# Second join and node stage in one pass, forward sums in the joins, first nodes' rows scattered during the lists

## The chip, the cores and the metric

The kernel runs on one core of a Trainium2 chip. The metric is the device time of one execution in microseconds (us). The engines are named as in the profile: PE (matmuls and transposes; PEld its weight loads), DVE (VectorE), ACT (ScalarE), POOL (GpSimd), SP (a queue that issues DMAs). Time before: 3021.86 us, the median of 3 runs (3020.35 to 3023.98).

## The reference, cut to what matters

```python
h = relu(x)                                        # 6250 nodes x 256
h = relu(gat_conv(h, src, dst, edge_attr, ...1))   # 106250 edges sorted by dst, 8 heads
h = gat_conv(h, src, dst, edge_attr, ...2)
x = h + x                                          # plus a mixing branch of the normalised x
# gat_conv: alpha = leaky_relu(a_src[src] + a_dst[dst] + a_edge); softmax over the edges of one dst;
#           out[dst] = sum(xp[src] * alpha) + bias
# then: y = layernorm(x); logits = relu(y @ rw1 + rb1) @ rw2 + rb2; the best two of 6 experts per
#       node, each a three-layer network of width 256; their weighted sum is added to x
```

The kernel computes all of it: two attention layers over the edges, the mixing branch, a router and the experts.

## The kernel before, in words

Edges are cut into T = 832 tiles of 128 (P), in the order of their destination, and nodes into 50 blocks of 128 or NCH = 25 chunks of 256 (CH). The kernel is a row of stages; each is a block in which every engine has an instruction list of its own, semaphores order the engines, and the next block starts when all have ended.

- `first`: layer norm of x, the rows of layer 1 (`table[0]`), and all constants, among them `begins` (1 where a tile's list starts anew for a destination), `ends_sep`, `ends_same` and `fix_rows`, the first destination of each tile. Small extra pieces are hung on DVE behind certain chunks (`pieces`).
- `edges` (twice): gathers a row for each edge, softmax within a tile, sums per destination into `acc`. Because a destination can lie on two or more tiles, each tile leaves its first and last destination's partial maximum and sum in `ends` and partial outputs in `parts`. In layer 2 this stage also leaves `base`, what has to be added to each node.
- `join` (twice): joins the partial results over tiles. PE picks `ends` into 8 rows (one a head) of L = 1664 entries (`pick`), ACT copies them out (`picked`), DVE scans forward and backward for the maxima (L1456, L1458), ACT takes the exponential (L1438), DVE makes `weight`, scans forward for the denominators and backward to carry the total to all entries (L1469, L1471), inverts, multiplies the outputs' parts by the weights (L1479), scans them forward (L1484), cuts (L1487), scans backward (L1489), copies (L1491), and multiplies by the inverse (L1496). Beside this the chunks of `acc` pass: ACT adds the bias (`biased`, L1413), PE projects them with the next layer's weights (layer 0) or only transposes them (layer 1), ACT copies rows (L1422), POOL splits the scores (layer 0) or adds `base` (layer 1, L1297), SP stores. PE's list puts the spreads (`spread`, L1334), which wait for DVE, between loops over chunks. Last come the first nodes of the tiles (`fix`): T rows in NFIX = 7 groups are projected (L1393), completed, and scattered over the stored rows by 7 indirect DMAs (L1314), which wait for all stores. A destination that is the first of several tiles is written several times, with the same values.
- `front`: the node stage. SP fetches a chunk of `node`, DVE takes its statistics (L1591, L1594), POOL the power -0.5 (L1583), DVE normalises both blocks (L1601), SP stores them, PE transposes (L1644), multiplies (L1653), and makes logits (L1660) with ACT's copies between; the router's weights are four small loads on ACT's queue.
- `dispatch`, the lists: the best two experts of a node, and for each expert the list of its nodes; SP loads the experts' weights and then stores two weights per node into `node` (L1741).
- `experts`: gathers the nodes' rows by these lists, runs the networks, scatters.

The order is written out by hand; no planner sets it.

## Time and profile before

| what | value |
|---|---|
| median of 3 runs | 3021.86 us |
| profiled execution | 3012.53 us, span 3010.7 us |
| mean granted PE clock | 0.892 of full speed |
| busy share of the span | PE 77%, DVE 72%, POOL 67%, ACT 39% |
| costliest group | POOL L702 (gathers for edges), 1583.6 us busy |
| second group | PE L1086 (sums over edges), 1106.0 us busy |

Busy time is the time in which an engine worked on instructions. "Idle before" stands in brackets behind a row of a timeline, with what ended it. Rows of a timeline begin with the start in us from the span's start and the busy time in us.

### The profile page before, as it was taken

To read this page: it belongs to the slowest core of one execution; us is meant where nothing else is said; L and a number is where in the kernel's file an instruction comes from. 1 tells how busy PE (TensorE), PEld (TensorE's weight loads), DVE (VectorE), ACT (ScalarE), POOL (GpSimd) and SP (SyncE) were. 2 spreads that over 40 slices of the span, in tenths; PEclk is the share of its full clock that TensorE was granted. 3 is DMA by queue.
4 is the path that set the end of the run, shared out by engine and by line. 5 is a ranking of instruction groups with operands and counts; after the bars stand their busy time and mean duration, and the time that the engine had idled before them with its cause. 6 is when DMAs were issued, how large, how long until landed. Compare 5 with 4: busy or idle time off the path is not lost. (4 is left out here: it accounts for less than half of the span.)

```text
span 3010.7 us, 76172 instructions
## 1 busy us (share of the span) xinstructions
PE 2320.1 (77%) x15555; PEld 1916.9 (64%) x15556; DVE 2170.8 (72%) x6026; ACT 1174.4 (39%) x4767; POOL 2026.9 (67%) x2248
## 2 busy tenths in 40 slices
PE   6577888888888888857777777777777756499897
PEld 4466666666666666636666666666666636387786
DVE  7477778777877777638777777777778686766565
ACT  3244444444444445413333333333333453322222
POOL 4577777777777775577777777777777473166665
PEclk9799999999999999868898898888889857599999
DMA  8765655555655553255655655665656356444432
GB/s 259 208 171 154 172 159 167 168 170 156 172 168 158 166 168 99 72 143 169 177 169 165 179 166 173 176 173 161 175 164 174 105 166 192 119 155 154 121 116 85
DMA packets 295431, 478.77 MB, mean 159 GB/s; under 512 B 69780, under 2 KB 211500, under 8 KB 295364
## 3 DMA queue, kind: packets, MB, share of 16 engines
q0 software_dynamic: 96704, 287.77, 33.6%
q1 hardware_dynamic: 134340, 143.68, 16.5%
q10 hardware_dynamic: 64320, 46.56, 4.9%
q8 instruction: 26, 0.43, 0.1%
q14 instruction: 41, 0.34, 0.0%
HBM read 405.02 MB, written 74.87 MB: 159 GB/s over the span
## 5 line engine op out<-in xcount | busy, mean ns | idle before, releaser
L702 POOL DMA_INDIRECT e_rows<-table,e_idx x1664 | 1583.6, 952 | 555.5 <-issue 396.5
L1086 PE MATMUL e_ps_sum<-e_hot,e_msg 128*128 128x129 f32 x6656 | 1106.0, 303 | 270.0 <-DVE e_msg L743 215.2
L1086 PEld LDWEIGHTS e_ps_sum<-e_hot,e_msg 128*128 128x128 f32 x6656 | 909.9, 203 | 429.2 <-ACT parts L941 239.5
L940 ACT ACTIVATE acc<-e_ps_sum 128x256 f32 x1664 | 640.5, 385 | 1222.2 <-PE e_ps_sum L1086 1036.7
L743 DVE TENSOR_TENSOR e_msg<-e_rows,e_ps_pr 128x256 f32<-128x256 f32 x1664 | 653.4, 413 | 80.6 <-issue 12.5
L722 DVE TENSOR_TENSOR e_hot<-e_ps_pr,rel 128x512 f32<-128x512 f32 x416 | 284.9, 685 | 160.0 <-PE e_ps_sum L1086 155.1
L1068 PE MATMUL e_ps_al<-e_dst_score,e_hotT 128*128 x3328 | 297.5, 179 | 1.1 <-issue 0.9
L1068 PEld LDWEIGHTS e_ps_al<-e_dst_score,e_hotT 128*128 128x128 bf16 x3328 | 248.3, 99 | 57.7 <-issue 1.8
L941 ACT ACTIVATE parts<-e_ps_sum 128x4 f32 (+1 forms) x1664 | 279.7, 168 | 0.0
L1075 PE MATMUL e_ps_al<-ident,e_lr 128*128 128x128 f32 x104 | 38.4, 369 | 176.3 <-DVE e_lr L767 175.2
L2042 ACT ACTIVATE x_h<-x,eb 128x128 f32<-128x128 f32 x216 | 67.6, 364 | 262.5 <-PE x L2111 262.5
L733 DVE TENSOR_SCALAR e_hotT<-e_relb,pcolf 128x512 bf16<-128x512 bf16 x416 | 155.3, 373 | 13.7 <-PE e_ps_al L1068 13.7
L733 DVE TENSOR_SCALAR e_hotT<-e_relb,pfar 128x512 bf16<-128x512 bf16 x416 | 151.8, 365 | 0.0
L1075 PEld LDWEIGHTS e_ps_al<-ident,e_lr 128*128 128x128 f32 x104 | 15.7, 151 | 195.9 <-DVE e_lr L767 195.9
L2111 PE MATMUL x<-x_h,x_w 128*128 128x128 f32 x864 | 124.6, 288 | 14.1 <-ACT x_h L2042 11.2
L2111 PEld LDWEIGHTS x<-x_h,x_w 128*128 128x128 f32 x864 | 107.9, 194 | 42.3 <-ACT x_h L2042 21.9
L2132 PE MATMUL x<-ew,x_h 128*128 x432 | 119.3, 399 | 19.9 <-DVE x_h L2070 19.6
L2111 PE MATMUL x<-x_yT,x_w 128*128 128x128 f32 x864 | 116.9, 279 | 5.4 <-ACT x_yT L2035 4.7
L2078 DVE TENSOR_TENSOR x_raw<-x,eb3b 128x256 f32<-128x256 f32 x108 | 45.8, 424 | 98.2 <-PE x L2132 98.2
L2111 PEld LDWEIGHTS x<-x_yT,x_w 128*128 128x128 f32 x864 | 106.9, 195 | 7.5 <-ACT x_yT L2035 6.6
L750 DVE COPY e_idx<-src_sb 128x16 int32 (+1 forms) x106 | 21.4, 203 | 123.6 <-DMA e_rows<-table,e_idx 123.2
L1095 PE MATMUL e_ps_a<-wkq,e_xT 128*128 128x512 f32 x200 | 108.3, 670 | 0.0
(322 smaller groups left out, 3419.6 us busy)
## 6 DMA issues: line engine op xcount, KB each, us to landing
e_relb<-rel_rows SPq DMA_DIRECT2D x104, 512.0 KB
e_rows<-table,e_idx POOLq DMA_INDIRECT x1664
e_eattr<-in_edge_b SPq DMA_DIRECT2D x104, 128.0 KB
e_xT<-turned_x ACTq DMA_DIRECT2D x100, 128.0 KB, 3.7
e_xr<-in_x ACTq DMA_DIRECT2D x100, 128.0 KB
table<-t_row SPq DMA_DIRECT2D x25, 276.0 KB, 4.0
table<-j_row SPq DMA_DIRECT2D x25, 276.0 KB, 2.4
e_mark<-marks SPq DMA_DIRECT2D x104, 64.5 KB
```

Source lines behind the costliest of these rows:

```text
L702: nc.gpsimd.indirect_dma_start(out=rows[q][:, k, :], out_offset=None, in_=table, in_offset=bass.IndirectOffsetOnAxis(ap=idx[:, q, k:k + 1] ...
L722: nc.vector.tensor_tensor(hot[:, q, 4 * r:4 * r + 4, 0:P], iota[c].unsqueeze(1).broadcast_to((P, 4, P)), rel[:, bass.ds(g * GT + 4 * r, 4) ...
L733: op = nc.vector.tensor_scalar(hotT[:, r % 2, far], relb[:, q, 4 * r:4 * r + 4, :], number[:, 0:1], None, ALU.is_equal)
L743: nc.vector.tensor_tensor(msg[:, k % RM, :].rearrange("p (h c) -> p h c", c=C), rows[q][:, k, 0:F].rearrange("p (h c) -> p h c", c=C), ps_ ...
L940: nc.scalar.activation(acc[:, :, bass.ds(at[k], P)], ps_sum[(k + q) % 3][:, :, 0:P], ACT.Copy).then_inc(s["window"], 1)
L941: nc.scalar.activation(parts[:, bass.ds(g * GT + k, 1)].rearrange("p t a b -> p (t a) b"), ps_sum[(k + q) % 3][:, :, 0:P + 1:P], ACT.Copy) ...
L1068: op = nc.tensor.matmul(parts_al[:, m, :], hotT[:, r % 2, far, k, :], pieces[:, bass.ds(b + far, 1), :].rearrange("p a c -> p (a c)"), sta ...
L1086: op = nc.tensor.matmul(ps_sum[(k + q) % 3][:, a, 0:WIN], msg[:, k % RM, a * P:a * P + P], hot[:, q, k, :], start=(a == 0), stop=True, ski ...
L1095: op = nc.tensor.matmul(ps_a[:], xT[:, q, a, :], wkq[:, a, :], start=(a == 0), stop=(a == 1))
L2042: op = nc.scalar.activation(h1[:, a, :], ps_1[q][:, a * P:a * P + P], ACT.Relu, bias=eb[:, 0, bass.ds(e, 1), a:a + 1].rearrange("p e a -> ...
L2111: op = nc.tensor.matmul(ps[k % 2][:, a * P:a * P + P], w[:, k % 2, m, h, a * P:a * P + P], of[:, h, :], start=(h == 0), stop=(h == 1))
L2132: op = nc.tensor.matmul(ps_3[k % 2][:, 0:F], h2[:, h, :], ew[:, 2, bass.ds(e, 1), h, :].rearrange("p e f -> p (e f)"), start=(h == 0), sto ...
```

## The change

It has four parts.

First, in both joins the sums over tiles run forward only: the backward scans of the denominators and of the outputs, the cut and the copy are gone. The total of a destination that lies on several tiles then stands only at the last of them. So `first` computes `fix_put`: for a tile whose first destination is also the first of the next tile the scatter goes to a spare row (NP + tile) and else to the destination's own row; `table[1]` and `node` have NFIX * P spare rows for this. The backward scan for the maxima stays.

Second, `join` now serves layer 0 only, and `last_join` takes the place of the second join and of `front`. It passes through `ORDER`, 29 steps: chunks 0 to 15, then four steps with the tiles' first nodes (two groups a step, the last with one of 64 rows), then chunks 16 to 24. In each step ACT adds the bias, PE transposes into one bank, ACT copies 128x512 in one operation, POOL adds `base`, DVE takes the statistics, POOL the power, DVE normalises the first block of the pair and POOL the second, PE transposes and multiplies for the router three to five steps later. SP stores a chunk's sums and normalised rows together, 512 KB, and fetches only `base`, into the half of the row buffer that the normalised rows overwrite later; there are six buffers. DVE's work of the join is cut into pieces that hang behind steps 0 to 8, with a last piece, `scale`, behind step 25. PE's spreads stand before steps 2, 5, 7 and 10. PE and ACT wait for the router's four small loads at the start (PE before its first pick).

Third, the logits of nodes that are a tile's first are put in by a product: `scale` makes for each group a table of 50 blocks by 7 columns, `replace` multiplies it with a 0/1 matrix of lanes (7 products of 350 columns), and the last operations on DVE multiply the chunks' logits by `keep`, add the replacements and the bias.

Fourth, the scatter of the tiles' first nodes (now rows of 528 columns with both sums and normalised rows) moves from the join's end into `dispatch` on POOL, and SP's store of the weights waits for it. The experts' weights `ew` now lie in the space of `acc`; they are loaded in `dispatch` as before.

```diff
+        table = [nc.dram_tensor(f"table{l}", (NP + l * NFIX * P, TW), F32).ap() for l in range(2)]
+        node = nc.dram_tensor("node", (NP + NFIX * P, MW), F32).ap()
...
         mid = nc.dram_tensor("mid", (NP, MW), F32).ap()
...
+        ew = acc[:].rearrange("p a n -> p (a n)")[:, 0:3 * NEXP * 2 * F].rearrange("p (m e a f) -> p m e a f", m=3, e=NEXP, a=2)
...
         dispatch(nc, sb, pb, sem, locals())
...
                 nc.vector.tensor_single_scalar(place_i[:], v["fix_rows"][:], P - 1, ALU.bitwise_and)
                 vec.drain()
                 nc.vector.tensor_copy(place[:], place_i[:])
+                nc.vector.tensor_copy(fixf[:, 0], v["fix_rows"][:])
+                nc.vector.tensor_tensor(fixf[:, 1], v["fix_rows"][:], fix_next[:], ALU.is_equal)
...
+                nc.vector.tensor_tensor(fixf[:, 2], inode[:, 0:NFIX], v["fix_rows"][:], ALU.subtract)
...
+                nc.vector.scalar_tensor_tensor(fixf[:, 1], fixf[:, 2], float(NP), fixf[:, 1], ALU.add, ALU.mult)
...
+                nc.vector.tensor_tensor(fixf[:, 0], fixf[:, 0], fixf[:, 1], ALU.add)
...
+                nc.vector.tensor_copy(v["fix_put"][:], fixf[:, 0])
...
-                    out=result, out_offset=bass.IndirectOffsetOnAxis(ap=fix_rows[0:n, f:f + 1], axis=0),
+                    out=result, out_offset=bass.IndirectOffsetOnAxis(ap=fix_put[0:n, f:f + 1], axis=0),
...
-            nc.vector.tensor_tensor_scan(top[:, ::-1], sep[0:H, 1:L + 1][:, ::-1], fwd[:, ::-1], -BIG, ALU.add, ALU.max)
-            vec.drain()
-            nc.vector.tensor_single_scalar(inv[:], top[:, 0:L:2], 1e-16, ALU.add)
+            nc.vector.tensor_single_scalar(inv[:], fwd[:, 0:L:2], 1e-16, ALU.add)
...
-                nc.vector.tensor_tensor_scan(b[:], same[:, 0:L], a[:], 0.0, ALU.mult, ALU.add)
-                vec.drain()
-
-                nc.vector.tensor_tensor(b[:], b[:], begins[:, 1:L + 1], ALU.mult)
-                vec.drain()
-                nc.vector.tensor_tensor_scan(a[:, ::-1], same[:, 1:L + 1][:, ::-1], b[:, ::-1], 0.0, ALU.mult, ALU.add)
-                vec.drain()
-                nc.vector.tensor_copy(total[:, half, :], a[:, 0:L:2])
+                nc.vector.tensor_tensor_scan(b[:, half], same[:, 0:L], a[:], 0.0, ALU.mult, ALU.add)
...
-                    op = nc.vector.tensor_tensor(total[:, half, f * Q:f * Q + Q], total[:, half, f * Q:f * Q + Q],
+                    op = nc.vector.tensor_tensor(total[:, half, f * Q:f * Q + Q], b[:, half, 2 * f * Q:2 * f * Q + 2 * Q:2],
...
+def last_join(nc, sb, pb, sem, v):
...
+    RX = 6
...
+    AT = 16
+    FIXED = [("fix", j) for j in range(-(-NFIX // 2))]
+    ORDER = [("row", c) for c in range(AT)] + FIXED + [("row", c) for c in range(AT, NCH)]
...
+        total = a[:].rearrange("p (h t) -> p h t", h=2)
...
+            def fetch(c):
+                if c >= RX:
+                    sp.wait_ge(s[f"out{c % RX}"], 16 * (c // RX))
+                    sp.wait_ge(s["yt"], upto(c - RX))
+                sp.dma_start(row[:, c % RX, :, F:2 * F], base[c * CH:c * CH + CH, :].rearrange("(b p) f -> p b f", p=P)
+                             ).then_inc(s[f"part{c % RX}"], 16)
...
+                fetch(c)
+            for c in range(NCH):
+                sp.wait_ge(s["yn0"], upto(c))
+                sp.wait_ge(s["yn1"], upto(c))
+                sp.dma_start(node[c * CH:c * CH + CH, 0:2 * F].rearrange("(b p) f -> p b f", p=P), row[:, c % RX]
+                             ).then_inc(s[f"out{c % RX}"], 16)
...
+            def norm(m):
...
+                pool.wait_ge(s["mv"], m + 1)
+                nc.gpsimd.tensor_tensor(rstd[0:n, m % 2, 0:k], eps[0:n, m % 2, 0:k], cst[0:n, 0:1].broadcast_to((n, k)), ALU.pow
+                                        ).then_inc(s["rstd"], 1)
+                pool.drain()
+                if k == 2:
+                    nc.gpsimd.tensor_scalar(place(m)[:, 1, F:2 * F], place(m)[:, 1, 0:F], mv[:, m % 2, 1, 0:1],
+                                            rstd[:, m % 2, 1:2], ALU.subtract, ALU.mult).then_inc(s["yn1"], 1)
...
+                kind, c = ORDER[m]
...
+                if kind == "row":
+                    pool.wait_ge(s[f"part{c % RX}"], 16 * (c // RX) + 16)
+                else:
...
+                nc.gpsimd.tensor_tensor(rows[:, :, 0:F], rows[:, :, 0:F], rows[:, :, F:2 * F], ALU.add).then_inc(s["sum"], 1)
+                if m > 0:
+                    norm(m - 1)
+            norm(NS - 1)
...
+            def replace():
...
+                                          scaled[0:n, f].rearrange("p b e -> p (b e)"), start=(f == 0), stop=(f == NFIX - 1))
+                op.then_inc(s["fixed"], 1)
...
+            pe.wait_ge(s["small"], 16 * 4)
...
+            spreads = {2: (0, 1, 2), 5: (3, 4, 5), 7: (6, 7, 8, 9), 10: (10, 11)}
+            for m in range(NS + 5):
+                for j in spreads.get(m, ()):
+                    spread(j)
+                if m < NS:
+                    project(m)
+                if 3 <= m < NS + 3:
+                    turn(m - 3)
+                if 4 <= m < NS + 4:
+                    hidden(m - 4)
+                if 5 <= m:
+                    logit(m - 5)
...
+            act.dma_start(rb2[:], v["rb2"].rearrange("(a f) -> a f", a=1).broadcast_to((P, NEXP))).then_inc(s["small"], 16)
...
+            biased(0)
+            for m in range(NS + 4):
+                if m + 1 < NS and ORDER[m + 1][0] == "row":
+                    biased(ORDER[m + 1][1])
+                if m < NS:
+                    rows(m)
+                if m == 0:
+                    act.wait_ge(s["less"], 1)
+                    nc.scalar.activation(ex[:], top[:], ACT.Exp).then_inc(s["ex"], 1)
+                if m == AT - 2:
+                    act.wait_ge(s["total"], 1)
+                    for h in range(2):
+                        op = nc.scalar.activation(total[:, h, :], total[:, h, :], ACT.Identity, bias=gbias[:, 1, h:h + 1])
+                    op.then_inc(s["fixT"], 1)
+                if 3 <= m < NS + 3:
+                    turned(m - 3)
+                if 4 <= m:
+                    rectified(m - 4)
...
+            def scale():
...
+                for f in range(NFIX):
+                    n = min(P, T - f * P)
+                    op = nc.vector.tensor_tensor(scaled[0:n, f], in_block[0:n, f].unsqueeze(2).broadcast_to((n, NB, KEEP)),
+                                                 of_fix[0:n, f].unsqueeze(1).broadcast_to((n, NB, KEEP)), ALU.mult)
...
+            steps = {0: weights, 1: denominators, 2: inverses, 3: lambda: products(0), 4: lambda: sums(0),
+                     5: lambda: products(1), 6: lambda: sums(1), 8: whole, AT + 9: scale}
+            lanes_of_fixed()
+            peaks()
+            moments(0)
+            for m in range(NS):
+                if m + 1 < NS:
+                    moments(m + 1)
+                normed(m)
+                if m in steps:
+                    steps[m]()
+            vec.wait_ge(s["small"], 16 * 4)
+            vec.wait_ge(s["fixed"], 1)
+            both = ps[0][:, 0:NB * KEEP].rearrange("p (b e) -> p b e", b=NB)
+            nc.vector.tensor_scalar(keep[:], both[:, :, NEXP], -1.0, 1.0, ALU.mult, ALU.add)
...
+            vec.wait_ge(s["lg"], NS)
+            nc.vector.tensor_tensor(logits[:], ps_l[:, 0:NB * NEXP].rearrange("p (b e) -> p b e", b=NB),
+                                    keep[:].unsqueeze(2).broadcast_to((P, NB, NEXP)), ALU.mult)
...
+            nc.vector.tensor_tensor(logits[:], logits[:], both[:, :, 0:NEXP], ALU.add)
...
+            nc.vector.tensor_tensor(logits[:], logits[:], rb2[:].unsqueeze(1).broadcast_to((P, NB, NEXP)), ALU.add)
...
+            sp.wait_ge(s_put, 16 * NFIX)
...
+            nc.gpsimd.memset(fix[:, :, 2 * F:MW], 0.0).then_inc(s_iota, 1)
+            pool.wait_ge(s_iota, 4)
+            for f in range(NFIX):
+                n = min(P, T - f * P)
+                nc.gpsimd.indirect_dma_start(
+                    out=node, out_offset=bass.IndirectOffsetOnAxis(ap=fix_put[0:n, f:f + 1], axis=0),
+                    in_=fix[0:n, f, :], in_offset=None).then_inc(s_put, 16)
+            pool.wait_ge(s_put, 16 * NFIX)
```

## Rows read from the trace of the kernel before

**Rows 1.** Busy time by stretch: first join, second join, node stage (us:us, length, engines, PEclk, DMA share, GB/s).

```profile
1205.00:1310.00 105.00, 80.61 (x316) 58.27 (x316) 52.31 (x39) 46.86 (x118) 61.83 (x134) 0.83 0.22 77
2402.00:2501.00 99.00, 53.46 (x202) 33.64 (x202) 62.84 (x31) 45.53 (x118) 65.25 (x39) 0.56 0.48 150
2504.00:2560.00 56.00, 48.36 (x300) 43.53 (x300) 44.05 (x177) 26.81 (x50) 19.60 (x26) 0.90 0.77 232
```

**Rows 2.** Timeline, DVE, first join (start, us, engine, line, op, operands, count).

```profile
1232.97 3.61 DVE L1471 TENSOR_TENSOR_SCAN j_top<-ends_sep,j_fwd 8x1664 f32<-8x1664 bf16 x1
...
1257.30 3.62 DVE L1484 TENSOR_TENSOR_SCAN j_b<-ends_same,j_a 128x1664 f32<-128x1664 bf16 x1
...
1267.33 2.08 DVE L1496 TENSOR_TENSOR j_total<-j_total,j 128x416 f32<-128x416 f32 x4
```

**Rows 3.** Timeline, first join: PE, ACT and POOL; in brackets idle before, and releaser.

```profile
1243.16 3.43 PE L1334 MATMUL j<-j_mx,hsel 8*128 8x416 f32 x8 [1.66 <-DVE j_a L1479]
...
1269.93 0.69 ACT L1422 ACTIVATE j_row<-j_row 128x272 f32<-128x272 f32 x2 [7.60 <-DMA table<-j_row]
...
1222.57 0.22 POOL L158 TENSOR_TENSOR j_row<-j_rest,j_row 128x16 bf16<-128x16 f32 x1
```

**Rows 4.** Timeline, start of the second join: PE, POOL and DVE.

```profile
2403.12 7.50 PE L1328 MATMUL j<-ends,ident 128*8 128x104 f32 x64 [4.31 <-PEq L69]
...
2407.35 0.95 POOL L1301 DMA_INDIRECT j_fix_part<-base,fix_rows  x1 [0.30 <-issue]
...
2408.27 3.61 DVE L1456 TENSOR_TENSOR_SCAN j_fwd<-ends_sep,j_mx 8x1664 f32<-8x1664 bf16 x1 [12.99 <-ACT j_mx L1404]
```

**Rows 5.** DMA issues by line, second join to lists (queue, size, median us to landing).

```profile
f_rb<-in_rb ACTq DMA_DIRECT2D x1, 3.0 KB, 4.2
```

**Rows 6.** Timeline, DVE, second join.

```profile
2419.26 5.75 DVE L1463 TENSOR_TENSOR j_mx<-j_fwd,j_sm 8x1664 f32<-8x1664 f32 x1 [1.73 <-ACT j_fwd L1438]
...
2436.90 5.34 DVE L1475 RECIPROCAL j_inv<-j_inv 8x832 f32<-8x832 f32 x1
...
2444.27 3.62 DVE L1484 TENSOR_TENSOR_SCAN j_b<-ends_same,j_a 128x1664 f32<-128x1664 bf16 x1
...
2469.94 2.08 DVE L1496 TENSOR_TENSOR j_total<-j_total,j 128x416 f32<-128x416 f32 x4
```

**Rows 7.** Timeline, POOL, second join: ten adds, and one alone.

```profile
2450.56 24.12 POOL L1297 TENSOR_TENSOR j_row<-j_row,j_part 128x512 f32<-128x512 f32 x10 [10.14 <-ACT j_row L1422]
...
2480.86 1.26 POOL L1297 TENSOR_TENSOR j_row<-j_row,j_part 128x512 f32<-128x512 f32 x1 [0.16 <-ACT j_row L1422]
```

**Rows 8.** Timeline, DVE and POOL, node stage.

```profile
2504.56 0.75 DVE L1591 BATCH_NORM_STATS2 f_stats<-acc 128x6 f32<-128x256 f32 x2 [15.21 <-DMA acc<-node]
...
2518.20 0.73 DVE L1601 TENSOR_SCALAR acc<-acc,f_mv,f_rstd 128x256 f32<-128x256 f32 x2
...
2518.37 0.79 POOL L1583 TENSOR_TENSOR f_rstd<-f_eps,cst 128x2 f32<-128x2 f32 x1 [1.08 <-DVE f_eps L1596]
...
2520.07 0.73 DVE L1601 TENSOR_SCALAR acc<-acc,f_mv,f_rstd 128x256 f32<-128x256 f32 x2
...
2559.20 0.47 DVE L1612 TENSOR_TENSOR logits<-f_l,f_rb 128x300 f32<-128x300 f32 x1 [4.86 <-PE f_l L1660]
```

**Rows 9.** Timeline, PE, node stage, its start and its even part.

```profile
2507.89 1.09 PE L1644 MATMUL f_y<-ident,acc 128*128 128x128 f32 x4 [20.73 <-DVE acc L1601]
...
2510.57 1.91 PE L1653 MATMUL f_r<-parts,f_rw 128*128 128x256 f32 x4
...
2514.84 0.81 PE L1660 MATMUL f_l<-f_rw,parts 128*128 128x6 f32 x4
...
2517.21 0.63 PE L1644 MATMUL f_y<-ident,acc 128*128 128x128 f32 x4
...
2518.91 0.63 PE L1644 MATMUL f_y<-ident,acc 128*128 128x128 f32 x4
```

**Rows 10.** Timeline, SP, lists: the weights' store.

```profile
2583.76 0.66 SPq L1741 DMA_DIRECT2D node<-d_weight  x1
```

More of the change, by code:

```diff
@@ L85, in sem @@
             return ctx.enter_context(nc.semaphore(name))
-        table = [nc.dram_tensor(f"table{l}", (NP, TW), F32).ap() for l in range(2)]
-        node = nc.dram_tensor("node", (NP, MW), F32).ap()
+        table = [nc.dram_tensor(f"table{l}", (NP + l * NFIX * P, TW), F32).ap() for l in range(2)]
+        node = nc.dram_tensor("node", (NP + NFIX * P, MW), F32).ap()
         rel_rows = nc.dram_tensor("rel_rows", (T, P), BF16).ap()
@@ L702, in gather @@
                     nc.gpsimd.indirect_dma_start(
-                        out=rows[q][:, k, :], out_offset=None, in_=table,
+                        out=rows[q][:, k, :], out_offset=None, in_=table[0:NP],
                         in_offset=bass.IndirectOffsetOnAxis(ap=idx[:, q, k:k + 1], axis=0)).then_inc(s[f"rows{q}"], 16)
@@ L2007, in _ @@
             for t in range(AHEAD):
-                fetch(t, node)
+                fetch(t, node[0:NP])
             for t in range(TT):
@@ L2016, in _ @@
                 if t + AHEAD < TT:
-                    fetch(t + AHEAD, node if t < TH else mid)
+                    fetch(t + AHEAD, node[0:NP] if t < TH else mid)
                 store(t)
```

582 lines of the change are left out of this document (352 added, 230 removed).

## The prediction

> **What bounds the kernel now.** I read the page's slices first, then busy time by stretch, then the timeline of each engine at the seams. About 2,190 of the 3,010.7 us of the profiled span are the two edge stages (up to the first join's start at 1,205 us, and from its end to the second join's start at 2,402 us); the change touches no instruction in them. What it touches is the first join, the second join, the node stage `front`, and a little of `first` and the lists [rows 1]. The reader is to see that the second join is bound by no engine: 63 of 99 us busy on DVE, 65 on POOL, 53 on PE at a granted clock of 0.56, that is mostly the lower level of 1.2 GHz. The node stage is bound by PE and DVE together (48 and 44 of 56 us, clock 0.90). Between the two lies a seam in which nearly nothing runs: DVE idles 15.21 us before its first statistics at 2504.56 [rows 8], because the first nodes' rows are projected, added and scattered after all others and the node stage then fetches back what was just stored. So the second join and the node stage take from 2,402 to 2,559.7 us, 157 us, one after the other.
>
> **First join, forward sums.** The change removes the backward scan for the denominators (3.61 plus a gap of 0.08: 3.7 us) and, in each half, the product, the backward scan and the copy between the end of L1484 (1257.30 + 3.62 = 1260.92) and L1496 at 1267.33, 6.4 us [rows 2]. DVE's chain is 3.7 + 2 × 6.4 = 16.5 us shorter. How much of it lies on the path? DVE ends its chain at 1,269 us and waits for rows later, so only what PE, ACT and POOL waited for counts: PE waited 1.66 us for the products, and ACT 7.60 us for a row buffer whose store waited for POOL [rows 3]. POOL was held back while DVE ran two-operand work. Both waits go: 9.3 us. The forward scans that stay can still hold POOL for 3.6 us each, covered by four row buffers; I subtract 0.8 and take 8.5. Bounds: 3.7 (only the denominators' scan counts) and 12. What is late next is PE, which has 80.6 busy of 105 us [rows 1]. The scatter keeps its seven issues; that it aims at other rows costs nothing.
>
> **Stage `first`.** Seven tiny DVE operations and one load of some KB. From the smallest POOL work, 0.22 [rows 3], I put them at 0.2 each: 1.4 us on a stage where DVE is late. I take 1, bounds 0 and 2.
>
> **Start of the merged stage.** Before, PE picked at once (2403.12) and DVE started scanning 5.15 later, at 2408.27 [rows 4]. Now PE waits for the router's four small loads, issued by ACT over 2 us behind which 4.2 us to landing stand [rows 5]: some 1.4 + 4.2 = 5.6 us later, so 2408.7, with six fetches of 256 KB before them on other queues (bounds 4 and 9). DVE's first scan is then at 2413.9. POOL's seven gathers at 1.25 each [rows 4] end at 2412.4, ahead of the scan. Two scans and a subtraction (9.3) and one POOL add let in between (1.3) end at 2424.5; ACT, which stands at `less`, does the exponential (1.9) and only then rows 1; POOL adds, DVE takes moments and does the weights, 5.75 + 1.9 when an add stood against it before [rows 6], 4 now by my reading. Step 0 ends at 2435.
>
> **Steps 1 to 8.** DVE per step: the node stage's cadence is 1.87 (2518.20 to 2520.07) with two normalisations in it [rows 8]; one goes to POOL, so 1.55 back to back, 1.7 with its waits: 8 × 1.7 = 13.6. To this come denominators 3.7, inverses 6.4 (5.34 the reciprocal, the rest 0.6 to 1.4), products 2 × 2.1, scans 2 × 3.7, the whole sums 2.1 [rows 6]: 23.8. Waits for the POOL operation in front of each scan, 3 × 0.8: 2.4. Sum 39.8, so step 8 ends at 2474.8. PE (2.2 per step plus twelve spreads of 0.86) and ACT are inside that.
>
> **Steps 9 to 28.** Here POOL decides. Per step it adds 128x512 (1.26 alone, 2.41 each when DVE scans: 24.12 for ten) [rows 7], powers (0.79) [rows 8], and normalises one block of 128x256, which the trace doesn't have on POOL. Its bounds are the operation on 16 columns, 0.22 [rows 3], and more than the whole add, 1.26, since two per-row scalars are read; by length it is 0.63, which I take. With a drain and two waits of about 0.1 each: 1.26 + 0.79 + 0.63 + 0.25 = 2.9 us (2.5 to 3.6). The other limits lie below it: DVE 1.7; PE 1.70 (2517.21 to 2518.91) [rows 9] plus four more transposes, 0.63 × 1.70 / 2.17 = 0.5, makes 2.2 at the upper clock; DMA moves 768 KB a step, which at the node stage's 232 GB/s for a share of 0.77 [rows 1] is 2.6 us at full share. The margin over DMA is small. 19 steps × 2.9 = 55.1. `scale` in step 25 takes the port for some 3 us. PE at the lower clock where the early steps leave gaps: 3 us, an allowance. Last normalisation: 2474.8 + 61 = 2535.9.
>
> The Trainium skill, "SBUF — State Buffer", section "Who interferes with whom", calls the port between DVE and POOL an exclusive lock. The trace agrees: the adds take 2.41 in place of 1.26 under the scans. By the rule alone an add fully blocked by each remaining scan would cost nothing new in the sum, for the scans stand in it; it speaks against the change only if the POOL normalisation were caught too, and DVE's per-row normalisation and pow overlap in the node stage at 0.79.
>
> **Tail.** Before, the logits came 4.86 us after DVE's last work [rows 8]; the same five steps stay. Then seven products of 350 columns replace the first nodes' logits: 3.43 for four spreads of 416 columns [rows 3] gives 0.72 each, 5.0 at the upper clock with little overlap; I take 4.5. DVE then has two operations of 0.47 more and gaps: 1.5. The last operation ends at 2535.9 + 4.9 + 4.5 + 1.5 = 2546.8 in place of 2559.7: 12.9 us earlier.
>
> **Lists.** Seven scatters at 1.25 from 2,560 on, landing 3 us later: 2,572, or 2,578 if DVE holds them up. The weights' store on SP is behind the expert loads and was issued only at 2583.76 [rows 10]; that cover hides them. Without that cover SP would store the weights late and the block could end later, by at most the 3 us of a landing. Cost 0, bounds 0 and 3. The renamed buffer for the experts and the slices cost nothing: the loads were issued in this block before too.
>
> **Sum.** 8.5 + 12.9 - 1 = 20.4 us off. The profiled execution took 3012.53 us (span 3010.7), 9.3 below the median of the runs, 3021.86. Against its own time: 2992.1. Against the median: 3001.5.
>
> **Rivals.** (A) POOL isn't 2.9 but 3.6 to 3.9 a step, since its normalisation costs as much as an add, or stores of 512 KB land late and SP's fetch waits behind them. For: DMA share 0.77 already. Against: six buffers. 19 × 0.85 = 16 us given back: 3017, no change within the noise. (B) The other side: PE holds the lower level. For: the second join with its transposes stood at 0.56, while the node stage rose only after PE had run without gaps from 2510. In the merged stage PE would have 4.4 us a step (double 2.2) instead of 2.2 and become the bound; it decides from a PE step above 2.9. Price 19 × 1.5 = 28.5, early steps 3, the tail 5: 3001.5 + 36.5 = 3038, slower than before. Against: at 4.4 PE has no gap, and that is what raised the clock in the node stage [rows 9]. The Trainium skill, "TensorE: Matmul & The Clock Gate", section "Part 4: PE-mode transpose", says that the upper level does not engage on transposes. Eight of the sixteen operations of a merged step are transposes, so the rule speaks for B; the node stage had four of twelve and reached 0.90. (C) More than I count: POOL's normalisation is 0.35, the first join gives 12: 19 × 0.3 + 3.5 = 9 more, 2992. (D) The overlap fails at the front: small loads late, the steps 0 to 8 serial on the port, 12 us lost: 3013.
>
> **How the numbers follow.** Chances: forecast 0.52 (own range 2994 to 3009), A 0.13, B 0.08, C 0.15, D 0.12. A difference of 0.2%, 6 us, is about what the measurement can tell, so faster is below 3015.8: forecast, C, D mostly (0.10) and a part of A (0.04), 0.81; within 0.2%: the rest of A and D, 0.11; slower 0.08. The range leaves out B and the far end of C: 2987 to 3019.
>
> **What would show it.** In the changed profile: L1469's successor in the first join directly the addition; no ACT wait of 7 us on `table`; first join near 96 us up to its end; PE's picks 5 to 6 us after the block's start; POOL back to back at 2.9 a step while DVE idles before its statistics for the sum; PEclk near 1 from the tenth step on; no idle seam before the node statistics; seven scatters done before the weights' store. The prediction is wrong if DVE or DMA has no idle in the even steps, if POOL's 128x256 takes over 1 us, if PEclk stays at 0.5, or if the edge stages move by more than 2 us each.

## The result, and the profile after

The changed kernel took 3030.17 us (median of 20 runs; the kernel before 3019.09, also of 20), a ratio of 1.004 with a 95% interval of 1.0032 to 1.0048: slower by 0.4%, some 12 us, where 20 us faster was forecast. The profiled execution took 3030.84 us (span 3029.0). Times by stage come from the two traces, each from the first instruction of a stage to the first of the next:

| stretch | before | after | difference | forecast |
|---|---|---|---|---|
| first pick to the next stage's first product | 116.3 | 106.7 | -9.6 | -8.5 |
| second join and node stage (first row gather to the lists' first operation) | 156.4 | 176.0 | +19.6 | -12.9 |
| lists (to the experts' first memset) | 47.1 | 47.15 | 0 | 0 |

The first join begins 4.7 us later in this execution (first pick 1211.24 against 1206.57). The two profiled executions lie 18.3 us apart (spans 3029.0 and 3010.7), more than the medians, because that of the kernel before was 6.6 us under its median; the medians decide on the whole time, the traces only on where it went. The miss lies in the merged stage: 32.5 us between forecast and trace.

Busy time by stretch of the changed kernel, to be set against [rows 1] (same columns: PE, PEld, DVE, ACT, POOL, granted clock, DMA share, GB/s): its first join, steps 0 to 9 of the merged stage, and the rest of it.

```profile
1209.00:1314.00 105.00, 77.66 (x320) 56.48 (x320) 42.30 (x52) 47.54 (x119) 58.15 (x140) 0.84 0.29 91
2399.00:2500.00 101.00, 52.23 (x222) 37.17 (x223) 55.50 (x107) 29.56 (x61) 51.44 (x38) 0.65 0.29 94
2500.00:2577.00 77.00, 54.43 (x341) 45.95 (x338) 35.77 (x127) 41.97 (x87) 59.17 (x60) 0.96 0.44 147
```

The second row is the one to look at. Three engines are busy half the time and ACT less, in a stretch that was meant to overlap them: they take turns. The timelines of the same stretch show whose turn it is. First PE (start, us, engine, line, operation, operands, count, idle before and its releaser):

```profile
2433.85 4.50 PE L1614 MATMUL l<-l_mx,hsel 8*128 8x416 f32 x6 [13.76 <-DVE l_mx L1802]
2438.27 1.97 PE L1632 MATMUL l_row<-ident,l_hT 128*128 128x128 f32 x8
...
2457.45 4.52 PE L1614 MATMUL l<-l_mx,hsel 8*128 8x416 f32 x6 [12.37 <-DVE l_a L1818]
2461.91 0.47 PE L1632 MATMUL l_row<-ident,l_hT 128*128 128x128 f32 x1
```

L1614 is the spread, L1632 the projection that stands behind it in PE's list. Now VectorE in the same stretch:

```profile
2441.41 0.75 DVE L1857 BATCH_NORM_STATS2 l_stats<-l_row 128x6 f32<-128x256 f32 x2 [7.71 <-POOL l_row L1585]
...
2465.04 0.75 DVE L1857 BATCH_NORM_STATS2 l_stats<-l_row 128x6 f32<-128x256 f32 x2 [5.21 <-POOL l_row L1585]
```

The ring is: a spread waits for VectorE's weights (13.76) or for a product that frees its bank (12.37); the projection waits in the queue behind it; ACT's rows wait for the projection, POOL's add for the rows, and VectorE's statistics (7.71, 5.21) for the add. VectorE, which is to free the spread, is among those that wait for the projection: the spread stands behind its piece of step m, and the projection of step m + 2, which stands behind the spread, feeds the next statistics in VectorE's list. By group over the merged stage (busy, mean ns of one | idle before, releasers):

```profile
L1585 POOL TENSOR_TENSOR l_row<-l_row 128x512 f32<-128x512 f32 x25 | 41.6, 1664 | 44.7 <-ACT l_row L1728 44.5 <-issue 0.3
...
L1857 DVE BATCH_NORM_STATS2 l_stats<-l_row 128x6 f32<-128x256 f32 x50 | 18.7, 414 | 47.6 <-POOL l_row L1585 47.6
...
L1728 ACT ACTIVATE l_row<-l_row 128x512 f32<-128x512 f32 x25 | 14.7, 589 | 46.6 <-PE l_row L1632 46.5
```

Each engine waits some 45 us for the one before it in that chain. From step 9 on the picture is another one; POOL's timeline of two steps:

```profile
2516.20 1.23 POOL L1572 TENSOR_SCALAR l_row<-l_row,l_mv,l_rstd 128x256 f32<-128x256 f32 x1 [0.19 <-issue]
2517.39 1.27 POOL L1585 TENSOR_TENSOR fix<-fix 128x512 f32<-128x512 f32 x1
2518.61 0.72 POOL L1568 TENSOR_TENSOR l_rstd<-l_eps,cst 128x2 f32<-128x2 f32 x1
2519.53 1.23 POOL L1572 TENSOR_SCALAR l_row<-l_row,l_mv,l_rstd 128x256 f32<-128x256 f32 x1 [0.19 <-issue]
```

From 2516.20 to 2519.53 a step is 3.33 us with POOL back to back: POOL is the bound, as forecast, but at 3.33 us and not 2.9, mostly since its normalisation takes 1.23 and not 0.63 (its power takes 0.72, the forecast had 0.79).

### The profile page after: what moved, and what is told of

The parts are those of the page before. It is cut to its first block and busy times, and to the rows that moved or that the text cites. A ratio compares the mean times of both kernels' runs of the same rounds, so it can differ in the third digit from the quotient of the medians.

```text
span 3029.0 us, 76098 instructions
## 1 busy us (share of the span) xinstructions
PE 2326.6 (77%) x15613; PEld 1925.1 (64%) x15614; DVE 2139.0 (71%) x6050; ACT 1173.8 (39%) x4747; POOL 2051.6 (68%) x2285
## 3 DMA queue, kind: packets, MB, share of 16 engines
q1 hardware_dynamic: 120884, 137.12, 15.6%
## 5 line engine op out<-in xcount | busy, mean ns | idle before, releaser
L758 DVE TENSOR_TENSOR e_msg<-e_rows,e_ps_pr 128x256 f32<-128x256 f32 x1664 | 653.1, 413 | 74.5 <-PE e_ps_sum L1101 10.3
L748 DVE TENSOR_SCALAR e_hotT<-e_relb,pcolf 128x512 bf16<-128x512 bf16 x416 | 151.0, 363 | 13.1 <-PE e_ps_al L1083 13.1
L2357 PEld LDWEIGHTS x<-x_h,x_w 128*128 128x128 f32 x864 | 107.7, 194 | 42.8 <-ACT x_h L2288 22.1
L2378 PE MATMUL x<-acc,x_h 128*128 x432 | 119.2, 399 | 20.2 <-DVE x_h L2316 20.1
```

The costliest lines, as they stand in the source:

```text
L748: op = nc.vector.tensor_scalar(hotT[:, r % 2, far], relb[:, q, 4 * r:4 * r + 4, :], number[:, 0:1], None, ALU.is_equal)
L758: nc.vector.tensor_tensor(msg[:, k % RM, :].rearrange("p (h c) -> p h c", c=C), rows[q][:, k, 0:F].rearrange("p (h c) -> p h c", c=C), ps_ ...
L2357: op = nc.tensor.matmul(ps[k % 2][:, a * P:a * P + P], w[:, k % 2, m, h, a * P:a * P + P], of[:, h, :], start=(h == 0), stop=(h == 1))
L2378: op = nc.tensor.matmul(ps_3[k % 2][:, 0:F], h2[:, h, :], ew[:, 2, bass.ds(e, 1), h, :].rearrange("p e f -> p (e f)"), start=(h == 0), sto ...
```

## The experiments

Twelve kernels ran, in three groups of four; the kernels of a group shared a chip and its runs of the kernel before. Ratios are to the kernel before; "stage" is the length in the trace of the merged stage (or of second join and node stage, where these were left), counted as in the table above. Four traces of the unchanged pair lie between 156.4 and 156.7 us, two of the merged stage at 174.7 and 176.0.

| kernel | ratio (95% interval) | stage, us |
|---|---|---|
| before, again | | 156.7 |
| added operations of `first` alone | 0.9995 (0.9977 to 1.0014) | 156.4 |
| forward sums in the first join alone | 0.9972 (0.9959 to 0.9984) | 156.6 |
| changed kernel, again | 1.0038 (1.0025 to 1.0050) | 174.7 |
| both blocks normalised on VectorE | 1.0010 (0.9997 to 1.0023) | 165.8 |
| spreads later | 0.9970 (0.9958 to 0.9982) | 152.7 |
| late wait for small loads | 1.0012 (0.9999 to 1.0025) | 166.0 |
| replacing products earlier | 1.0037 (1.0024 to 1.0051) | 175.4 |
| the three edits of PE's list | 0.9932 (0.9914 to 0.9951) | 141.5 |
| all four, exponential later | 0.9913 (0.9894 to 0.9932) | 133.4 |
| scaling and replacing products earlier still | 0.9929 (0.9905 to 0.9953) | 135.2 |
| scatters at the end of the stage | 1.0041 (1.0023 to 1.0059) | 176.6 |

My theory: the order of PE's list (spreads ahead of projections), the wait for small loads, and POOL's normalisation cost the time. The rivals: PE's low clock, and the port that VectorE and GpSimd share.

**The first join by itself.** The changed kernel with the second join, the node stage and the lists of before.

```diff
-            if layer == 0:
-                join(nc, sb, pb, sem, locals())
+            (join if layer == 0 else second_join)(nc, sb, pb, sem, locals())
...
-        last_join(nc, sb, pb, sem, locals())
+        front(nc, sb, pb, sem, locals())
```

> The first join with forward sums alone (with the few operations that work out its scatter rows); the second join and the last node stage are those of before, the scatter of the first nodes too. Theory: the first join's gain is real and independent of the rest, the -9.65 us between the two traces, less about 1 us for the added operations: time 8 to 10 us under the kernel before (near 3010), and the stretch from the first pick to the next stage's first table operation about 97.6 us instead of 107.2. Then the merged stage alone costs some 20 us. Rival: the 4.7 us by which the first join starts later in the trace of the changed kernel is a price of the part too (the operations in the first stage), so that the sum is only 3 to 5 us under before; second rival: the gain comes from how the changed kernel lies in memory or in time and is not seen here (0 us).

Measured: 0.9972, 8.5 us under before, and 104.9 us from the first pick to the next stage's first product (before 116.3). The gain of this part is real and stands alone, so the merged stage costs about 20 us by itself. (The other traces with forward sums have this stretch at 104.3 to 109.6 us, those without at 116.3 to 116.8.)

**Both blocks normalised on VectorE.**

```diff
-                if k == 2:
-                    nc.gpsimd.tensor_scalar(place(m)[:, 1, F:2 * F], ...).then_inc(s["yn1"], 1)
...
+                for k in range(blocks):
+                    op = nc.vector.tensor_scalar(place(m)[:, k, F:2 * F], place(m)[:, k, 0:F], mv[0:n, m % 2, k, 0:1],
+                                                 rstd[0:n, m % 2, k:k + 1], ALU.subtract, ALU.mult)
```

> The changed kernel with both blocks of a chunk normalised on VectorE; GpSimd has only the add and the power. Theory: GpSimd's 3.33 us a step (1.27 + 0.72 + 1.23 and gaps) bounds steps 9 to 28, VectorE has 1.6 us idle in each of them, so the step falls to about 2.2 us: 20 x 1.1 = 22 us, perhaps 3 us less for the two-block steps during the join: 18 to 22 us under the changed kernel, so near 3009. Rival (the shared port): VectorE's longer work makes the adds 1.9 us and more, the step stays at 2.8 to 3 us: 7 to 10 us under the changed kernel. Rival (PE or the stores bound the step at once): no more than 5 us.

Measured: 1.0010 against 1.0038, 8 to 9 us under the changed kernel, its stage 9 us shorter: by the number the second of the three cases, not mine. Busy time in 40 us of the even part, first the changed kernel, then this one:

```profile
2510.00:2550.00 40.00, 27.50 (x191) 23.65 (x192) 19.32 (x72) 25.80 (x56) 37.53 (x37) 1.00 0.51 165
```

```profile
2510.00:2550.00 40.00, 34.25 (x243) 30.10 (x241) 35.00 (x107) 33.16 (x72) 31.46 (x32) 1.00 0.65 214
```

POOL falls from 37.5 to 31.5 of 40 us, and the step from 3.33 to about 2.5 in this stretch (16 powers in 40 us); from the normalisation of step 9 to the last it is 2.76 on average, 3.32 in the changed kernel. VectorE goes from 19 to 35. By an estimate from these rows some 6 us of that come from steps that follow each other faster (16 in the place of 12), some 5 from the second block (16 x 0.33, the pair taking 0.73 and one block 0.40), and the rest, some 4, from its smallest operation, which is stretched while POOL adds:

```profile
2526.38 1.21 DVE L1852 TENSOR_SCALAR l_eps<-l_mv 128x2 f32<-128x2 f32 x1
...
2529.29 0.17 DVE L1852 TENSOR_SCALAR l_eps<-l_mv 128x2 f32<-128x2 f32 x1
```

The same operation takes 0.17 alone and 1.21 beside POOL's add, and where it overlaps an add it ends 0.02 to 0.03 us after the add's end. The rival of the port named the right size but another way to it: POOL's adds, which were to take 1.9 us and more, take 1.27 in these steps, and it is VectorE that is held. How much of the new step is this and how much VectorE's own work isn't separated. The tenth power begins where it did (98.0 us after the stage's start, 97.6 in the changed kernel): the steps up to there were not bound by POOL.

**Spreads later**, one iteration on, and behind the iteration's projection and turn.

```diff
-            spreads = {2: (0, 1, 2), 5: (3, 4, 5), 7: (6, 7, 8, 9), 10: (10, 11)}
+            spreads = {3: (0, 1, 2), 6: (3, 4, 5), 8: (6, 7, 8, 9), 11: (10, 11)}
             for m in range(NS + 5):
-                for j in spreads.get(m, ()):
-                    spread(j)
                 if m < NS:
                     project(m)
                 if 3 <= m < NS + 3:
                     turn(m - 3)
+                for j in spreads.get(m, ()):
+                    spread(j)
```

> The changed kernel with the twelve spreads issued one iteration later on PE, and behind that iteration's project and turn instead of ahead of its project. Theory: in steps 0 to 8 PE stands in front of a spread that waits for VectorE while the projection that would feed GpSimd's next add stands behind it in PE's queue (VectorE idle 7.7, 5.2, 5.2, 3.0, 2.4 us for the add, 23.6 us in all); moved behind, those projections run ahead: 12 to 20 us under the changed kernel, VectorE's waits for the add under 1.5 us each in steps 1 to 8. Rival (PE's low clock in the gaps makes spreads and projections slow, 1.48 instead of 0.86 us a spread): the order changes nothing, the spreads still cost 1.4 to 1.5 us each, and the time is within 4 us of the changed kernel. Rival (one lock between VectorE's scans and GpSimd's adds): within 4 us too, with the same adds of 2.4 us and more.

Measured: 0.9970 against 1.0038, 20 us under the changed kernel; the stage 22 us shorter. What the spreads waited for, in the changed kernel and then in this one (durations as ns min/median/max):

```profile
L1614 PE MATMUL l<-l_mx,hsel x16: 507/896/1057, 2433.8 to 2474.5; 8*128 8x416 f32 x16
...
its engine sat idle before it (us, times) until:
  DVE l_a L1818: 35.8, 6
  issue: 17.6, 11
  DVE l_mx L1802: 13.8, 1
  DVE l_a L1832: 11.5, 2
```

```profile
L1614 PE MATMUL l<-l_mx,hsel x16: 507/896/1057, 2436.6 to 2466.4; 8*128 8x416 f32 x16
...
its engine sat idle before it (us, times) until:
  issue: 4.8, 18
  DVE l_a L1818: 0.3, 1
  DVE l_a L1832: 0.2, 1
```

The waits for VectorE (61 us, weight loads and products counted together) are gone, and the median of the spreads' records (two to a spread) is 896 ns in both: the same low clock, another order. That the clock was the cause of these 20 us falls with this. It is not out of the picture: in this kernel PE hardly stops in the steps up to 9, and its clock is still low there (busy time of PE, PEld, DVE, ACT, POOL, granted clock, DMA):

```profile
2440.00:2460.00 20.00, 16.09 (x50) 10.50 (x49) 16.82 (x26) 5.89 (x13) 15.56 (x12) 0.59 0.44 141
2460.00:2480.00 20.00, 20.00 (x88) 15.32 (x88) 16.20 (x33) 11.65 (x25) 16.93 (x13) 0.73 0.47 151
```

Steps 1 to 8 take 45.0 us here instead of 61.9, and PE is busy 41.1 of the 45.0, more than VectorE (36.7): it is now the busiest engine of these steps. What its low clock costs there was not tested. The groups that waited 45 us each, in this kernel:

```profile
L1585 POOL TENSOR_TENSOR l_row<-l_row 128x512 f32<-128x512 f32 x25 | 36.7, 1467 | 16.0 <-ACT l_row L1728 15.6 <-issue 0.3
...
L1857 DVE BATCH_NORM_STATS2 l_stats<-l_row 128x6 f32<-128x256 f32 x50 | 18.7, 414 | 22.9 <-POOL l_row L1585 22.1 <-issue 0.3 <-DVE l_a L1832 0.2
```

15.6 instead of 44.5, and 22.1 instead of 47.6. What is left in VectorE's early waits is the start (3.05 us ahead of chunk 1, and 1.1 to 1.2 twice).

**The small loads.** PE's wait for them stands ahead of the first hidden product, ACT's ahead of the first rectification, instead of ahead of the picks and the first bias.

```diff
-            pe.wait_ge(s["small"], 16 * 4)
             for what in range(2):
                 for f in range(4):
                     pick(what, f)
...
+                if m == 4:
+                    pe.wait_ge(s["small"], 16 * 4)
                 if 4 <= m < NS + 4:
                     hidden(m - 4)
```

> The changed kernel with PE's wait for the router's four small loads moved from ahead of the picks to ahead of the first hidden product, and ScalarE's from ahead of the first bias to ahead of the first rectification. Theory: in the changed kernel PE's first pick stood 12.9 us for the load that lands last, and VectorE's first scan began 14.4 us after the stage's first gather against 4.7 us in the kernel before; without the wait the first scan starts 5 to 7 us earlier and everything behind it by as much: 5 to 7 us under the changed kernel, near 3026. Rival (the picks, 8.85 us at the low clock, and the four DMA issues on ScalarE set the start in any case): 0 to 2 us. Rival (the steps behind are bound by PE's order, which a shorter start does not shift): 0 to 2 us with an early first scan.

Measured: 1.0012 against 1.0038, 8 us; the stage 9 us shorter, more than I gave it. PE's first picks in the changed kernel, and in this one:

```profile
2408.39 8.85 PE L1598 MATMUL l<-ends,ident 128*8 128x104 f32 x64 [12.88 <-DMA l_rb<-in_rb]
```

```profile
2398.15 8.44 PE L1598 MATMUL l<-ends,ident 128*8 128x104 f32 x64 [4.16 <-PEq L69]
```

Against the stage's first gather they start 8.1 us after it and now 0.6 ahead of it. The forecast counted the landing from the row of the old node stage, 4.2 [rows 5]; beside the six fetches of 256 KB the last of the four loads took 6.4 (5.3 to 7.0 in seven other traces of the merged stage).

**The replacing products**, three iterations before the end of PE's list in place of behind it.

```diff
                 if 5 <= m:
                     logit(m - 5)
-            replace()
+                if m == NS + 1:
+                    replace()
```

> The changed kernel with the seven products that put the first nodes' logits into place issued three iterations before the end of PE's list instead of behind its last. Theory: VectorE's last four operations wait 12.06 us for PE, 4.57 of which are these products; their operands are there from step 25 on, so the stage ends 3.5 to 4.6 us earlier: near 3029. Rival (moved forward they delay the turns of the last steps by the same 4.6 us, PE being the bound of the tail): under 1 us.

Measured: 1.0037, the same as the changed kernel. The rival is right: the products were only moved ahead of the last turn, the last two hidden layers and the last three logits, which PE still had to do. PE in this kernel's tail:

```profile
2567.50 1.12 PE L1643 MATMUL l_y<-ident,l_row 128*128 128x128 f32 x4 [4.41 <-DVE l_row L1870]
...
2573.56 4.56 PE L1675 MATMUL l<-l_b,wext 128*128 128x350 f32 x14
2578.05 0.66 PE L1643 MATMUL l_y<-ident,l_row 128*128 128x128 f32 x4
```

The bound of the tail is PE from 2567.5 on, behind VectorE's 4.2 us of `scale` and with its first four transposes at 1.12 instead of 0.66.

**The three edits of PE's list together** (the last three diffs), POOL still normalising.

> Later spreads, late wait for the small loads and early replacing products together (the three edits of PE's list), GpSimd still normalising the second block. Theory: the losses lie in three places that follow each other in time, so the gains add: 22 + 6 + 4 = 32 us under the changed kernel (27 to 34), about 3001, 19 us under the kernel before. Rival (with the spreads later, the 1.23 us normalisation on GpSimd and the longer scans under the lock bound the stage from the start, and the earlier start is lost again): 22 to 26 us.

Measured: 0.9932, 20.5 us under before and 32 under the changed kernel (by the ratios); the stage 141.5 us, 33.8 shorter than the mean of the two traces of the changed kernel. The gains add up (22.6 + 9.3 in the stage; the earlier replacing products added at most 2). This kernel reaches the time that the prediction had forecast for the change.

**All four edits**, and ACT's exponential behind the rows of chunk 1.

```diff
-                if m == 0:
+                if m == 1:
                     act.wait_ge(s["less"], 1)
```

> The three edits of PE's list, both blocks normalised on VectorE, and ScalarE's exponential one step later, behind the second chunk's rows. Theory: another 8 to 14 us under the kernel with the three edits (normalising on VectorE alone gave 8.6 us; the step was then 2.6 us instead of 3.33, the rest being VectorE's waits of up to 1.2 us for the port and PE's chain): about 2990, 28 to 32 us under before. Rival (VectorE is the bound of steps 0 to 8 once the spreads don't hold it up, and the second block's 0.37 us a step and its scans' waits make these longer): 3 to 6 us only.

Measured: 0.9913 (26 us under before), with the three edits 0.9932; the intervals overlap, but the traces have the stage at 133.4 instead of 141.5 us, the low end of the 8 to 14 us expected. Which of the two added edits brought it was not separated. It has the lowest ratio and the shortest stage of this study. Busy time in 40 us of its even part:

```profile
2465.00:2505.00 40.00, 34.88 (x244) 30.05 (x244) 36.43 (x110) 33.38 (x72) 30.88 (x31) 1.00 0.67 218
```

VectorE is busy 36.4 of 40 us, PE 34.9, ACT 33.4: there is little left to overlap.

**Scaling and replacing products earlier still**: `scale` at step 23, the products at iteration 27.

```diff
-                     5: lambda: products(1), 6: lambda: sums(1), 8: whole, AT + 9: scale}
+                     5: lambda: products(1), 6: lambda: sums(1), 8: whole, AT + 7: scale}
...
-                if m == NS + 1:
+                if m == NS - 2:
                     replace()
```

> The kernel with all four edits, and in it VectorE's 4.2 us of scaling the first nodes' logits at step 23 instead of 25 and the seven replacing products before the last three iterations of turns rather than in their midst. Theory: PE's tail behind the last normalisation (15.1 us in the kernel with all four) loses the 4.4 us stall that lets its clock fall and the 4.6 us of products: 3 to 6 us under that kernel, 30 us under before. Rival (VectorE is busy 88 % of the stage and carries the 4.2 us in any place; PE then catches up no sooner): within 2 us of it.

Measured: 0.9929, stage 135.2 us: no gain, by the trace 1.8 us worse. Neither theory named the reason. The products, 5.68 us at this place, now stand ahead of the last projection, and VectorE waits for the chain behind it:

```profile
3414.92 5.68 PE L1667 MATMUL l<-l_b,wext 128*128 128x350 f32 x14
3420.52 0.66 PE L1625 MATMUL l_row<-ident,l_hT 128*128 128x128 f32 x4
```

```profile
3423.20 0.75 DVE L1850 BATCH_NORM_STATS2 l_stats<-l_row 128x6 f32<-128x256 f32 x2 [7.65 <-POOL l_row L1578]
```

The last normalisation then ends 8.2 us later in the stage than in the kernel with all four, and the tail behind it is 6.4 us shorter, so the tail gained what was expected and the steps before it lost more. It is the fault of the spreads a second time, made by me; this is read from the trace, no run moves the products alone.

**The scatters back at the end of the stage.** GpSimd waits there for the last stores and scatters the seven tiles; the lists have none.

```diff
             norm(NS - 1)
+            for q in range(RX):
+                pool.wait_ge(s[f"out{q}"], 16 * len(range(q, NCH, RX)))
+            for f in range(NFIX):
+                nc.gpsimd.indirect_dma_start(out=node, ..., in_=fix[0:n, f, :], in_offset=None).then_inc(s["put"], 16)
+            pool.wait_ge(s["put"], 16 * NFIX)
```

> The changed kernel with the seven scatters of the first nodes' rows put back to the end of the merged stage's list on GpSimd (behind the last store), instead of in the lists. Theory: GpSimd is done 13 us before the stage ends (it waits for PE's and VectorE's tail), so seven issues of 1.25 us and a landing of 2 us start about 4 us into that gap and end at about its end: 0 to 3 us over the changed kernel, so moving the scatter into the lists brought almost nothing here. Rival (the whole of the scatter is exposed, as the 15.2 us in which VectorE waited between the two stages of the kernel before suggests): 9 to 12 us over the changed kernel.

Measured: 1.0041 against 1.0038 of the changed kernel; stage 176.6 us against 176.0 and 174.7, lists 47.1. POOL's timeline: the scatters run from 3466.16 on, and the lists' first operation comes at 3477.68.

```profile
3466.16 1.15 POOL L1597 DMA_INDIRECT node<-fix,fix_put  x1 [3.82 <-DMA node<-l_row]
...
3473.95 0.90 POOL L1597 DMA_INDIRECT node<-fix,fix_put  x1 [0.30 <-issue]
3477.68 0.14 POOL L1996 IOTA d_pcol<- 128x1 int32 x1 [2.82 <-POOLq L1474]
```

POOL has nothing else to do in the tail, so the scatter is hidden there but for its end: moving it into the lists brought at most 2 us in this kernel.

**The added operations of `first`, and the kernel before once more.** The first is the kernel before with these lines of the change and no others:

```diff
+                nc.vector.tensor_copy(fixf[:, 0], v["fix_rows"][:])
+                nc.vector.tensor_tensor(fixf[:, 1], v["fix_rows"][:], fix_next[:], ALU.is_equal)
...
+                nc.vector.tensor_copy(v["fix_put"][:], fixf[:, 0])
```

> The kernel before with nothing but the added load and the seven added VectorE operations of the first stage that work out the scatter rows. Theory (they cost about 1 us, and the 4.7 us by which the first join starts later in the changed kernel's trace are mostly differences between executions): within 2 us of the kernel before, first pick within 3 us of 1206.6. Rival (they delay the start of all that is behind the first stage): 3 to 5 us over before, first pick near 1211.

> The kernel before once more, for a second execution of it in the profile: how far the start of its first join (1206.6 us in the first) moves between executions. Theory: by 3 us and more, as four executions of kernels with the same first two stages have it at 1209.7 to 1216.1. Rival: within 1 us.

Measured: ratio 0.9995. These two belong to the third group, in which everything took 3.9 ms (last section); first picks there at 1702.0 with the added operations and 1712.3 without. In the first two groups and the result's trace, seven kernels with the operations and the changed kernel twice have theirs between 1209.2 and 1216.1, all of them later than the one trace of the kernel before (1206.57). The start of the first join moves by several us from one execution to the next; a price of these operations, up to the 6 us that the interval leaves, isn't seen. There is no second trace of the kernel before at that speed, so the 4.7 us of the two traces stay open at that size, and the question put to the second trace of the kernel before isn't answered, since that trace is of the third group.

The changed kernel once more, unedited, in the first group:

> The changed kernel itself, as the one with which the others of this chip are compared: 10 to 12 us over the kernel before.

Measured: 1.0038, the result again.

## Why the prediction was wrong

**What bounds the kernel now**: right. The seam and the overlapping work were there to be had, as the stage of 133.4 us against 156.4 shows.

**First join**: right, -9.6 against -8.5. The waits named are gone: at PE's spreads (1246.12, no idle), and ACT's longest for `table` is 0.81 instead of 7.60 [rows 3]. What is late next is PE, as forecast.

**Stage `first`**: 1 us forecast, not distinguishable from 0 (the interval of the run with these operations alone reaches from 9 us faster to 6 us slower).

**Start of the merged stage**: right in kind, too small. The first scan came 14.4 us after the stage's start, forecast 10.3, before 4.7 [rows 4]. Of the 4.1 us the late landing (6.4 instead of 4.2) is 2.2, and 1.2 is the longer way from first pick to first scan (6.3 us instead of 5.15, the picks taking 8.85 instead of 7.50). The cost of the wait was 9 us by the stage of the kernel without it, not 5.6. Step 0 ended 2 us late.

**Steps 1 to 8**: here it failed. The step that failed was "PE (2.2 per step plus twelve spreads of 0.86) and ACT are inside that." It compared PE's total with VectorE's total and never asked what stands in front of what. PE executes one list in order; in it a spread that waits for VectorE's piece of step m stands ahead of the projection of step m + 2, whose statistics are what VectorE's list has next. Steps 1 to 8 took 61.9 us where 39.8 was forecast, in the kernel with later spreads 45.0 and in the one with all three edits 44.3: of the 22 us too many the order is 17. VectorE's sum was about right (35.0 us busy, forecast 37.4 without its waits). PE's was not: 8 x 2.2 + 12 x 0.86 is 28 us, and it was busy 37.7: 2.2 was taken at the upper clock, and the granted clock was 0.67 here. So in size too PE was not inside VectorE's sum. The 5 us by which 45.0 exceeds the forecast may be its price; no run shows that apart.

The forecast has the end of step 8 at 71.2 us after the stage's start (2474.8 - 2403.6); it came at 95.3. From there it counts 19 steps for steps 9 to 28, which are 20, so its sum fits the traces only if 71.2 is read as the end of step 9's normalisation. That ended at 99.8; with the spreads behind the projections it ended at 78.3, with all three edits at 67.5. Up to here the forecast missed 28.6 of the 32.5 us: 2 up to the end of step 0, 22 in steps 1 to 8, and 4.5 in the step that it didn't count.

**Steps 9 to 28**: the mechanism (POOL bounds) was right, the size wrong. The normalisation of 128x256 on POOL was taken at 0.63 by length and measured 1.23, near its upper bound of 1.26; the step is 3.33. That it takes over 1 us was one of the prediction's own signs of being wrong. From there to the last normalisation the trace has 63.1 us, forecast 61. That is about 19 x 3.33: on balance neither `scale` nor PE's clock added to it, so the 6 us allowed for these paid for most of the longer step. That this part came out near its forecast is luck. Rival A's cause (a normalisation as dear as an add) came to pass, without its price.

**Tail**: 13.1 us against 10.9. The replacing products took 4.57 (4.5 forecast); the rest is PE's list behind `scale`, where PE stood idle 4.41 us and then took 1.11 for four transposes that take 0.63 before.

**Lists**: right; 47.15 us, and the scatters were hidden. That they were hidden in the tail as well was not seen.

**Rivals**: B, the slower side, gave the right sign for a reason that held only in part. The granted clock was 1.00 from 2510 to 2550, with eight of a step's sixteen operations transposes. The Trainium skill, "TensorE: Matmul & The Clock Gate", section "Part 4: PE-mode transpose", says that the upper level does not engage on transposes; these steps show it engaged. Up to step 9 the clock was 0.65 on average, nearer the lower of its two levels, as B had feared for all steps; but the spreads kept their 896 ns when the 20 us went. D named the place (steps 0 to 8 serial) and blamed the port; it gave 12 us for what cost some 30, and its chance was 0.12. The Trainium skill, "SBUF — State Buffer", section "Who interferes with whom", calls the shared port an exclusive lock. The trace agrees: the 0.17 us operation takes 1.21 beside an add and ends with it. The port is no cause of the 20 us: in the kernel with later spreads as many of GpSimd's operations (four) are stretched beside scans as in the changed kernel.

## What to carry over

When two stages become one, write out each engine's list and go through it in order: for every instruction that waits, what stands behind it on its engine, and does the engine it waits for need any of that? Two sums of busy time that fit inside each other show nothing if the answer is yes; and where an engine will have gaps, take PE's sum at its lower clock too. Here moving twelve small products one iteration on, behind two projections, was worth more (20 us) than the merge was forecast to bring (12.9). And a semaphore wait belongs ahead of the first instruction that reads the data, not at the head of the list.

## What the runs showed of the hardware

- GpSimd's operation with two per-row scalars on 128x256 takes 1.23 us, as long as its two-input add of 128x512 (1.27); VectorE does the same block in 0.40 (changed kernel).
- While VectorE scans, the same operation on GpSimd takes 3.80 (two times in the kernel with later spreads), and an add 4.29. Each of these ends 1.03 to 1.07 us after the scan, so most of it seems to run behind the scan.
- The other way round, VectorE's operation on 128x2, 0.17 us alone, takes up to 1.21 beside GpSimd's add of 128x512 and ends 0.02 to 0.03 us after the add (both blocks on VectorE). Beside GpSimd's normalisation it takes 0.25 to 0.29 (changed kernel).
- In the third group the granted clock was 0.75 over the span instead of 0.90, and the kernel before took 3931 us; the record gives the same chip number for the second group, in which the kernel before took 3012 us, and what made the difference isn't shown. The 900 us more lie in the edge stages (clock 0.73 in 390 us of the first, against 0.95); the second join and node stage took 156.7 us against 156.4. Ratios of that group are over a longer total, so the same number of us is a smaller ratio in it: its 0.9929 is 28 us.
